# A two-layer graph attention kernel: in the second layer the probability is written into the one-hot, and TensorE sums the gathered rows themselves

## What is computed

```
q, k, v = x @ wq + bq, x @ wk + bk, x @ wv + bv
scores = sum(q[dst] * k[src]) / 16 + edge_weight * we + be
exp_s  = exp(scores - segment_max(scores, dst)[dst])
attn   = exp_s / segment_sum(exp_s, dst)[dst]
out    = segment_sum(v[src] * attn[:, None], dst)
x      = layer_norm(x + out + x @ ws + bs), then a feed-forward net and another layer norm
```

## Time and profile before

| | us |
|---|---|
| median of 3 runs | 8353.09 (8341.91 to 8355.75) |
| the profiled execution's own time | 8343.48 |
| its span, first to last instruction | 8341.3 |
| busy in the span: PE, DVE, POOL | 4585.1, 4170.8, 3716.7 |
| busy in the span: PEld, ACT | 3639.8, 2519.5 |
| mean granted clock of PE | 0.733 |

### The profile page before, as it was taken

How to read it: one execution, slowest core, us unless ns; L and a number is a source line. 1 busy time by engine, 2 the same in 40 slices (tenths; PEclk the granted TensorE clock), 3 DMA queues, 4 the chain that set the end, 5 groups by cost and what they waited for, 6 DMA issues and landing times. The chain is left out here.

```text
span 8341.3 us, 128676 instructions
## 1 busy us (share of the span) xinstructions
PE 4585.1 (55%) x27082; PEld 3639.8 (44%) x27082; DVE 4170.8 (50%) x13687; ACT 2519.5 (30%) x6512; POOL 3716.7 (45%) x3951
## 2 busy tenths in 40 slices
PE   5454545554555554556555555555555555555688
PEld 2344444444444444444333344444434344444477
DVE  5454545554545555547644444444444444444578
ACT  1343433443443444443112222222222222222232
POOL 1444444444444444441254445444444444444344
PEclk8676666666666667668877777777777777777799
DMA  5454445444455445443344545555544444455422
GB/s 153 136 136 131 133 132 137 132 137 132 133 133 137 132 132 137 131 134 96 117 130 125 124 121 130 121 123 125 125 117 128 120 123 120 126 123 123 115 70 66
DMA packets 847437, 1041.75 MB, mean 125 GB/s; under 512 B 286127, under 2 KB 598400, under 8 KB 846736
## 3 DMA queue, kind: packets, MB, share of 16 engines
q1 hardware_dynamic: 536000, 501.80, 23.4%
q0 software_dynamic: 169040, 436.01, 20.3%
q10 hardware_dynamic: 141696, 97.92, 3.7%
HBM read 931.22 MB, written 129.77 MB: 127 GB/s over the span
## 5 line engine op out<-in xcount | busy, mean ns | idle before, releaser
L582 POOL DMA_INDIRECT rows<-x_d,idx x1760 | 1801.7, 1024 | 1971.0 <-ACT msg L681 1390.2
L582 POOL DMA_INDIRECT rows<-kv_d,idx x1760 | 1679.2, 954 | 2071.6 <-DVE msg L1053 1259.5
L1276 PE MATMUL ps<-msg,oh 128*128 128x132 f32 (+1 forms) x7040 | 1840.9, 418 | 1171.8 <-issue 537.8
L1276 PEld LDWEIGHTS ps<-msg,oh 128*128 128x128 f32 x7040 | 1397.2, 243 | 1457.0 <-issue 836.7
L1276 PE MATMUL ps<-qw,oht 128*128 128x128 bf16 (+2 forms) x12320 | 1466.8, 268 | 938.6 <-issue 829.5
L1276 PEld LDWEIGHTS ps<-qw,oht 128*128 128x128 bf16 x12320 | 1127.8, 113 | 1337.3 <-issue 1053.3
L927 DVE CUSTOM_DVE_ANT_0 prod<-rows,ps 128x256 f32<-128x256 f32 x1760 | 636.3, 417 | 1237.6 <-remote 886.9
L680 ACT ACTIVATE msg<-rows,prob 128x256 f32<-128x256 f32 x1760 | 747.4, 496 | 1359.2 <-issue 844.7
L911 DVE TENSOR_TENSOR prod<-rows,ps 128x512 f32<-128x512 f32 x440 | 299.7, 681 | 1320.8 <-remote 1255.0
L1276 PE MATMUL ps<-w_c,ea 128*128 128x128 f32 x3520 | 681.1, 341 | 330.2 <-issue 300.2
L1077 DVE SCALAR_TENSOR_TENSOR acc<-acc,keep_tab,ps 128x132 f32<-128x132 f32 (+1 forms) x770 | 318.2, 413 | 937.6 <-remote 722.4
(11 more groups left out here) (199 smaller groups left out, 4358.3 us busy)
## 6 DMA issues: line engine op xcount, KB each, us to landing
dst_row<-in_dst_row SPq DMA_DIRECT2D x880, 256.0 KB
qw<-q_d SPq DMA_DIRECT2D x440, 192.8 KB
acc_d<-acc ACTq DMA_DIRECT2D x440, 128.5 KB
ea<-in_eaT SPq DMA_DIRECT2D x440, 128.0 KB
qw<-q_d SPq DMA_DIRECT2D x440, 96.0 KB
acc_d<-acc ACTq DMA_DIRECT2D x440, 66.0 KB
rows<-kv_d,idx POOLq DMA_INDIRECT x1760
rows<-x_d,idx POOLq DMA_INDIRECT x1760
```

The source lines that it names most:

```text
L582: pool.indirect_dma_start(out=rows[par][:, st, j, :], out_offset=None, in_=L.table, in_offset=bass.IndirectOffsetOnAxis(ap=idx[par][:, st, ...
L1276: return pe.matmul(out_, lhsT=lhsT, rhs=rhs, start=first, stop=last)
```

## The change

In layer 2 the probability is no longer multiplied into the rows. DVE makes the one-hot with four `tensor_scalar` of 128 columns, each `(iota == rel) * prob` with two scalars per partition, in place of one comparison over 512 columns. ACT's five instructions a step are gone, and with them `msgp` in that layer. PE multiplies this weighted one-hot by the gathered rows in place; for the sum of the probabilities each row gets a 257th column of ones beside it, which POOL writes once ahead of the layer, so a row takes 257 places of 4 bytes in SBUF. The buffers are now read until the matmuls are done, so the gathers wait for `agg` in place of `msgp`. Layer 1 keeps its instructions, with its message tile cut to 132 columns.

```diff
-        rows = [sb(f"rows{b}", [P, CH, JT, D]) for b in range(2)]
+        space = [sb(f"rows{b}", [P, CH * JT * (D + 1)]) for b in range(2)]
+        kv_rows = [r[:, 0:CH * JT * D].rearrange("p (s j n) -> p s j n", s=CH, j=JT) for r in space]
+        x1_rows = [r[:, :].rearrange("p (s j n) -> p s j n", s=CH, j=JT) for r in space]
...
-        msg = [sb(f"msg{b}", [P, JT, D + 1]) for b in range(OHS)]
+        msg = [sb(f"msg{b}", [P, JT, DM + HEADS]) for b in range(OHS)]
...
-                        after(pool, s["msg" if L is L0 else "msgp"], CH * (c - 2) + st + 1)
+                        after(pool, s["msg" if L is L0 else "agg"], CH * (c - 2) + st + 1)
...
-                                out=rows[par][:, st, j, :], out_offset=None, in_=L.table,
+                                out=L.rows[par][:, st, j, 0:D], out_offset=None, in_=L.table,
...
             end_phase(pool, 3)
+            for b in range(2):
+                pool.memset(space[b][:, CH * JT * D:CH * JT * (D + 1)], 0.0)
+            pool.drain()
+            for b in range(2):
+                pool.memset(x1_rows[b][:, :, :, D], 1.0)
+            pool.drain()
             gathers(L1)
...
                 def messages(c, par, st):
-                    pr = prob[par][:, st * JT:(st + 1) * JT, 0:L.H]
                     wait(s["agg"], CH * c + st - OHS + 1)
-                    if L is L0:
...
-                    else:
-                        for j in range(JT):
-                            act.activation(msg[st % OHS][:, j, 0:D], rows[par][:, st, j, :], ACT.Copy, scale=pr[:, j, :])
-                        act.activation(msg[st % OHS][:, :, D:D + 1], pr, ACT.Copy).then_inc(s["msgp"], 1)
...
-                        for r in L.summed[st] if sums else ():
+                        for r in L.summed[st] if sums and L is L0 else ():
                             messages(past, pp, r)
...
                     after(v, s["agg"], g - OHS + 1)
+                    v.wait_ge(s["prob"], c + 1)
                     if L is L0:
-                        v.wait_ge(s["prob"], c + 1)
...
                     else:
-                        v.tensor_tensor(oh[:, st % OHS, :, :], iota_row[:, :].unsqueeze(1).to_broadcast([P, JT, P]),
-                                        rel[par][:, st, :].unsqueeze(2).to_broadcast([P, JT, P]), ALU.is_equal)\
-                         .then_inc(s["msg"], 1)
+                        for j in range(JT):
+                            i = v.tensor_scalar(oh[:, st % OHS, j, :], iota_row[:, :], rel[par][:, st, j:j + 1],
+                                                prob[par][:, st * JT + j, 0:1], ALU.is_equal, ALU.mult)
+                        i.then_inc(s["msg"], 1)
...
                     pe.wait_ge(s["msg"], g + 1)
-                    pe.wait_ge(s["msgp"], g + 1)
+                    if L is L0:
+                        pe.wait_ge(s["msgp"], g + 1)
                     after(pe, s["acc"], g - 1)
                     for j in range(JT):
-                        i = mm(agg_ps(L, b), oh[:, st % OHS, j, :], msg[st % OHS][:, j, 0:L.AW], j == 0, j == JT - 1)
+                        i = mm(agg_ps(L, b), oh[:, st % OHS, j, :],
+                               msg[st % OHS][:, j, :] if L is L0 else x1_rows[par][:, st, j, :], j == 0, j == JT - 1)
                     i.then_inc(s["agg"], 1)
```

More of the change, by code:

```diff
@@ L182, in build @@
         rescale = sb("rescale", [P, HEADS])
-        msg = [sb(f"msg{b}", [P, JT, D + 1]) for b in range(OHS)]
+        msg = [sb(f"msg{b}", [P, JT, DM + HEADS]) for b in range(OHS)]
         acc = [sb(f"acc{b}", [P, D + 1]) for b in range(ACCS)]
         acc_scaled = sb("acc_scaled", [P, D + 1])
-        space = [r[:, :, :, :].rearrange("p s j n -> p (s j n)") for r in rows]
-        used = [0] * len(rows)
+        used = [0] * len(space)
         def slot_buffers(*shape):
@@ L193, in slot_buffers @@
             for b in range(U):
-                size, half = int(np.prod(shape)), b % len(rows)
+                size, half = int(np.prod(shape)), b % len(space)
                 buf = space[half][:, used[half]:used[half] + size]
@@ L287, in build @@
         L0.QD, L1.QD = DM, D + 1
+        L0.rows, L1.rows = kv_rows, x1_rows
         L0.summed, L1.summed = SUMMED
@@ L672, in messages @@
                 def messages(c, par, st):
-                    pr = prob[par][:, st * JT:(st + 1) * JT, 0:L.H]
                     wait(s["agg"], CH * c + st - OHS + 1)
-                    if L is L0:
-                        act.activation(msg[st % OHS][:, :, 0:L.AW].rearrange("p j (h c) -> p j h c", h=HEADS)[:, :, :, OUTC],
-                                       pr, ACT.Copy).then_inc(s["msgp"], 1)
-                    else:
-                        for j in range(JT):
-                            act.activation(msg[st % OHS][:, j, 0:D], rows[par][:, st, j, :], ACT.Copy, scale=pr[:, j, :])
-                        act.activation(msg[st % OHS][:, :, D:D + 1], pr, ACT.Copy).then_inc(s["msgp"], 1)
+                    act.activation(msg[st % OHS][:, :, :].rearrange("p j (h c) -> p j h c", h=HEADS)[:, :, :, OUTC],
+                                   prob[par][:, st * JT:(st + 1) * JT, :], ACT.Copy).then_inc(s["msgp"], 1)
                 def store(c, st):
@@ L902, in add_edges @@
                     v.wait_ge(s["e"], CH * c + st + 1)
-                    kv = rows[par][:, st, :, :].rearrange("p j (m n) -> p j m n", m=2)
+                    kv = kv_rows[par][:, st, :, :].rearrange("p j (m n) -> p j m n", m=2)
                     v.tensor_tensor(kv, kv, e_ps(b).rearrange("p (j n) -> p j n", j=JT).unsqueeze(2)
@@ L910, in products @@
                     half = prod[:, :, st % 2 * DM:(st % 2 + 1) * DM]
-                    v.tensor_tensor(half, rows[par][:, st, :, 0:DM],
+                    v.tensor_tensor(half, kv_rows[par][:, st, :, 0:DM],
                                     q_ps(L, st % 2).rearrange("p (j n) -> p j n", j=JT), ALU.mult)
@@ L927, in dots @@
                         i = v.tensor_tensor_reduce(
-                            out=prod[:, j, :], in0=rows[par][:, st, j, :], in1=q_ps(L, b)[:, j * D:(j + 1) * D],
+                            out=prod[:, j, :], in0=x1_rows[par][:, st, j, 0:D], in1=q_ps(L, b)[:, j * D:(j + 1) * D],
                             scale=1.0, scalar=0.0, op0=ALU.mult, op1=ALU.add,
@@ L1049, in weigh @@
                     after(v, s["agg"], g - OHS + 1)
+                    v.wait_ge(s["prob"], c + 1)
                     if L is L0:
-                        v.wait_ge(s["prob"], c + 1)
-                        m = msg[st % OHS][:, :, 0:L.AW].rearrange("p j (h c) -> p j h c", h=HEADS)[:, :, :, 0:OUTC]
-                        v.tensor_tensor(m, rows[par][:, st, :, DM:2 * DM].rearrange("p j (h c) -> p j h c", h=HEADS),
+                        m = msg[st % OHS][:, :, :].rearrange("p j (h c) -> p j h c", h=HEADS)[:, :, :, 0:OUTC]
+                        v.tensor_tensor(m, kv_rows[par][:, st, :, DM:2 * DM].rearrange("p j (h c) -> p j h c", h=HEADS),
                                         prob[par][:, st * JT:(st + 1) * JT, :].unsqueeze(3)
```

## The result

The kernel after takes 7840.4 us (median of 4 runs, 7837.9 to 7858.4) against 8354.4 (8341.9 to 8356.6): a ratio of 0.9385, interval 0.9364 to 0.9407. That is 514 us less. The forecast was 194 us less, and its range went from 7930 to 8460, so the result lies 90 us outside it. The profiled execution has a span of 7836.1 us, against 8341.3.

What follows compares the result with a forecast made beforehand. Bound: engines stopped by GpSimd's long gather bursts in layer 2. A chunk of 43.3 + 1.6 + 20.4 = 65.3 us against 69.0, over 54 chunks -200 us, +3 for memsets, gave 8160 us; range 7930 to 8460.

Steps and rivals of the forecast that it cites:

- What bounded the kernel: Layer 2's edge phase: no engine full; GpSimd's gather bursts stop the other engines about 8 us in, in 69.0 us chunks.
- The formula: Layer 2 chunk: W plus, for each gather burst, its length less 8 us; 25.7 us lost before the change.
- ScalarE, 0 on the path: Layer 2 messages removed: 959 us of ScalarE's busy time goes, worth nothing directly on the path.
- VectorE, +1.6 us a chunk: Layer 2 one-hot as four instructions: +0.2 us a pair, times 8, added to W; bounds +1.0 and +3.0 a chunk.
- the upper bound of 0.38: Layer 2 one-hot: four instructions end to end at 0.266 us, 1.06 us, so +0.38 us a pair at most.
- W: Layer 2 chunk: the work engines do when they are let, 43.3 us of 69.0, paced by DVE.
- TensorE, 0: Layer 2 matmuls: `rows` replaces `msg`, 8 matmul records a pair before and after, one wait fewer: cost 0.
- GpSimd, from 25.7 to 20.4 us lost a chunk: Layer 2 gathers wait for `agg`: bursts of 16 and 12 lose 12.8 + 7.6 us, a third of 4 loses 0.
- The rival that had the finer cut: Layer 2 gathers: engines stop with only `agg(2)` out, bursts 12, 12, 4, 4, 60.1 us a chunk, 7870 us; chance 0.17.
- Rival 2: Layer 2 gathers: pauses this short give nothing back, only the DVE term is left, +86 us, 8440 us; chance 0.20.
- Rival 3: Layer 2: the ring closes through GpSimd, gathers start 3.1 us later, +4.7 us a chunk, 8610 us; chance 0.11.
- Rival 4: Layer 2: DVE's short one-hots hold up GpSimd's gathers, +3.2 us a chunk, about no change, 8330 us; chance 0.07.

Runs made afterwards that it cites:

- e2: Kernel before; in layer 2 GpSimd also waits ahead of each even step until the previous step's gathers have landed: 7633 us, ratio 0.9142.
- e3: Kernel after with a coarser `agg` gate in layer 2, so that gathers come in bursts of 20 and 12 again: 8260 us, ratio 0.9878.
- e1: Kernel before with one edit: layer 2's gathers wait for `agg` instead of `msgp`; messages and old one-hot stay: 7822 us, ratio 0.9363.
- e8: Kernel after with ScalarE's old load put back in layer 2 as copies that nobody reads or waits for: 7813 us, ratio 0.9417.
- e4: Kernel after with the one-hot made by one comparison over 512 columns, the probability left out of the sums: 7848 us, ratio 0.9377.
- e5: Kernel after; layer 2 waits for landing ahead of each even step, a pause after every 8 gathers: 7561 us, ratio 0.9111.
- e6: Kernel after; layer 2 waits for landing ahead of every step, a pause after every 4 gathers: 8313 us, ratio 1.0028.
- e10: Kernel before with the wait for landing ahead of each even step in both layers, pauses after 8 gathers: 7121 us, ratio 0.8592.
- e12: Kernel after with pauses after every 8 gathers in both layers, and layer 1's gathers waiting for `agg` too: 7115 us, ratio 0.8583.
- e9: Kernel after with coarse gate (bursts of 20 and 12), layer 2's gathers bringing 64 of 256 columns: 8186 us, ratio 0.9875.
- e14: Kernel after with three memsets, each with a drain, on GpSimd ahead of each even step of layer 2: 7826 us, ratio 0.9345.

## Why the prediction was wrong in size

*What bounded the kernel.* Right: the stretch between GpSimd's gathers and the stop of the other engines. e2 and e3 show it from both sides. That no engine was full made the other parts cheap, and they were. The formula, for each burst its length less 8 us, is a good count of the loss too, as the table below shows.

*ScalarE, 0 on the path.* Right (e1, e8). Its busy time fell by 773 us, not 959: the 959 added durations that overlap their neighbours.

*VectorE, +1.6 us a chunk.* Wrong twice. The four instructions take 1.11 us in the timeline against 0.68, +0.43 us a pair, above the upper bound of 0.38; the row nearest in shape, with one scalar and one partition, was at 266 ns and the real one is at 354. The estimate from the Trainium skill ("VectorE: DVE Perf Modes", the TRN2 errata section), 0.51 us for the four, is under half of the 1.11 measured. And on the path no cost of it can be seen (e4, with its longer bursts, and the pairs named there), where the sum put its full size into W.

*TensorE, 0.* Right: e1 has the messages and the separate wait, and the same time within the intervals.

*GpSimd, from 25.7 to 20.4 us lost a chunk.* This is the step that failed. The trend was right (`agg` comes later and one by one, step 7 makes a burst of its own in the long pause). But "GpSimd runs out of free buffers at 12 to 16 gathers" supposed two to four steps' matmuls to be done and seen when the engines stop. In the trace GpSimd sees two: the burst is 8, it waits 2.5 us for a sum that PE had already recorded, and in that pause the engines move again. So the 28 gathers are cut in three, 8, 12 and 8, where the prediction had two and said that the cut hardly matters. With the prediction's own formula 8, 12, 8, 4 gives 2.4 + 7.6 + 2.4 + 0 = 12.4 us lost, in place of 20.4. Not every chunk is cut so. The formula put on every burst between 4300 and 6900 us, us a chunk:

| | bursts | formula's loss | chunk | what is left, W |
|---|---|---|---|---|
| before | 2.3 | 24.9 | 68.6 | 43.7 |
| e3 | 2.2 | 25.3 | 67.2 | 41.9 |
| e4 | 3.5 | 16.9 | 59.6 | 42.7 |
| e1 | 3.9 | 14.7 | 58.8 | 44.1 |
| after | 4.0 | 13.4 | 59.2 | 45.8 |
| e2 | 4.3 | 9.3 | 55.6 | 46.3 |

From before to e1 the loss falls by 10.2 us and the chunk by 9.8, so the formula carries the gate's whole gain once the bursts are counted right. In after the loss falls by 11.5 and the chunk by 9.4. Whether the 2.1 us between them are the longer one-hot (8 x 0.43 = 3.4) or the formula's error isn't shown; W strays by 2 to 3 us in the other rows too, and the formula knows nothing of GpSimd's own round, which binds in e5 and e6. The mechanism was right, and the number of bursts was wrong: two for 28 gathers, with a third for the last 4, where the runs have four a chunk. The rival that had the finer cut (12, 12, 4, 4, 7870 us) came within 30 us of the result. It had the right number of bursts with other lengths: its loss (15.2 us) was 1.8 above the one counted and its W (44.9) 0.9 below, so a part of that nearness is luck.

*Rival 2* read the chunks of 20, 4 and 8 at 70.5 us as short pauses that give nothing back. e2 refutes it. What those chunks share with the ordinary ones is the burst of 20. *Rival 3*, the later start, costs nothing to be seen (e1; e10 against e12). *Rival 4*, gathers held up by DVE's short instructions, did not come: the gather's mean went from 1024 to 1003 ns, and it is 1024 again in e4 with the single instruction. The rule of the Trainium skill that the rival named ("SBUF — State Buffer", SBUF: two separate sides) would speak for a hold-up; the rows show none that grows.

*What the prediction could have had.* The trace of before had bursts of 8 and 12 beside those of 20 in the same kernel. Between 4300 and 6900 us of it there are 13 bursts of 8, 16 of 12 and 21 of 20. PE, DVE and ScalarE are all idle for 1.3 us in one of 8, 4.0 in one of 12 and 13.5 in one of 20 (mean, to 1 us behind the last gather). So the loss grows faster than the burst, and the gain hangs on the cut more than on anything else that the diff touches.

## What to carry to other kernels

When an engine that issues gathers runs ahead of the others, look at the length of its bursts before its busy share: here 20 in a row stopped all the other engines for 13.5 us, and the same 32 gathers in four bursts of 8, in both layers, took 14% off the whole kernel. Then price the pauses: a wait for landing is about 3.3 us, so the issuer's own round (32 x 1.30 + pauses) must stay under what the other engines need. And where a change touches a synchronisation beside its work, run the synchronisation alone: the one word of e1 was all of this change's gain.

## What the runs showed of the hardware

- Long runs of indirect gathers stop PE, DVE and ScalarE (13.5 us with all three idle in a burst of 20), though by the code these gathers bring rows for the next chunk (the profile puts one of DVE's waits down to them, 9.08 us in the earlier trace rows), and a quarter of the bytes stops them as much (e9, 127 and 86 GB/s at the same pace). What in the chip does it is open: GpSimd's issuing, the rows' transfers, how semaphores come through, or how instructions reach the engines. That GpSimd itself sees PE's `agg` late (2.47 us, "remote") speaks for more than one engine's trouble. That PE's matmuls come a microsecond apart where no wait stands between them speaks for more than semaphores.
- Pauses of some 3 us after every 8 gathers are enough to let the engines go on (2.67 us in e2's lines).
- DVE waits 3.2 to 4.5 us before its first instruction of every second pass, in the kernel before as in after, where the hardware loop starts a new turn (3.25 and 3.54 us in the lines above). That the loop causes it is read from its place; no run changes the loop.
- A drain on GpSimd behind its gathers and a memset took 1.8 us at the median of e14 (2.88 in the lines above), and drains between memsets next to nothing.
- A DVE `tensor_scalar` of 128 x 128 fp32 with two per-partition scalars and two operations is 354 ns; four in a row take 1.11 us, where one `tensor_tensor` of 128 x 512 takes 0.68.
